# Embedding look-ups as fp32r matmuls over a table in two parts, with moved transposes and partial sums

## The chip, the cores and the metric

The kernel runs on one core of a Trainium2 chip. The metric is the device time of one execution in microseconds. The engines are TensorE (PE, matmuls into PSUM), VectorE (DVE), ScalarE (ACT), GpSimd (POOL, which also issues the gathers) and SyncE (SP, which issues the other transfers). Each runs its own instructions in order and waits on semaphores for the others.

## The reference

A recommendation tower over B = 512 samples: 40 look-ups in tables of 64 columns, one bilinear form for each of the 780 pairs of fields, then three dense layers. Cut to what matters:

```python
e = jnp.stack([tbl_0[ids[:, 0]], ..., tbl_39[ids[:, 39]]], axis=1)      # 512 x 40 x 64
vi, vj = e[:, i_idx, :], e[:, j_idx, :]                                 # 780 pairs i < j
z = jnp.einsum('bpe,bpe->bp', jnp.einsum('bpd,pde->bpe', vi, W), vj)    # 512 x 780
h = jnp.concatenate([z, dense_ctx], axis=1)                             # 512 x 796
h = jnp.maximum(h @ W_top1 + b_top1, 0.0)
h = jnp.maximum(h @ W_top2 + b_top2, 0.0)
y = h @ W_top3
```

## The kernel before

Fields are taken in 20 pairs; `x[:, k, :]` holds pair k transposed, one field in the lower 64 partitions, the other in the upper 64, samples along the free axis. Eight fields with tables of 1000 rows are the one-hot fields, pairs 0, 2, 4, 6. The rest are gathered: GpSimd issues 8 gathers a pair (two fields by four blocks of 128 samples, L396), with a memset of `spacer` (L391) and a wait for it between any two, and TensorE transposes the four blocks into PSUM (L559).

A one-hot look-up (`look`, L533 to L545) multiplies the table, in 8 blocks of 128 rows, with a one-hot matrix. VectorE makes that matrix by comparing the ids, copied to all partitions, with the row numbers (`make_rows`, L472, L484; 8 comparisons a field, two fields together). The two fields of a pair go to the two halves of the columns, so 16 matmuls of 128x64 by 512 in fp32. `one_hot` holds one pair.

Work on the forms is a list of 195 steps (`UNITS`): for k = 1, 2, ... all pairs m < k with k (`cross`, L606), some `inner` ones (L612), and from k = 8 on `rows` units (L595) which serve the pairs in `KEPT` from the other side. A step is two matmuls of 64 rows side by side into one of three `y_ps` slots, a product on VectorE with `x[:, k]` (L518) or `kept` (L504), and for every four summed steps a sum over partitions on TensorE three steps later (`sum_round`, L629). A product of a `rows` unit is summed by ScalarE in 16 activations (`sum_rows`, L440).

The order is written out. `plan_jobs` gives each step the jobs that come before it on every engine: `look`, `turn` (transposes), `mix` (ScalarE swaps halves for an inner unit), `partial` (the first layer's sum over z banks already finished, L574) and `z_turn`. `EARLY_JOBS` places the first ones by hand, the others stand `LEAD` = 5 steps ahead of their first use; `FIRST` is {5: 11, 6: 16, 7: 22, 8: 30, 9: 36, 10: 44, 11: 52} for these pairs. `ROWS_AT` places the comparisons on VectorE, ahead of a step's product. The results of jobs land in banks of `y_ps` for those of step 0 (`TURN_BANK`) and later in the one bank `t_ps`; the next job there waits until the last is copied out, by ScalarE (`copy_turn`, L409) or, for the second group of partial sums, by VectorE (L491):

```python
if TURN_BANK[n] in TURN_BANK[:n]:
    wait_turn_done(pe, max(i for i in range(n) if TURN_BANK[i] == TURN_BANK[n]))
```

In step 84 stand the transposes of pair 14 and partial sum (0, 0) together. SyncE loads ids and tables of the one-hot fields, 256 KB each, then chunks of weights.

## Time and profile before

| | |
|---|---|
| median of 3 runs | 351.81 us (351.06 to 351.86) |
| the profiled execution, its own time | 351.51 us |
| its span, first to last instruction | 349.7 us |
| TensorE busy | 331.0 us, 95% |
| VectorE busy | 258.4 us, 74% |
| ScalarE busy | 220.7 us, 63% |
| GpSimd busy | 153.8 us, 44% |
| granted TensorE clock | 1.00 |

Busy time of TensorE is that of matmuls whose ends are modelled: a busy engine isn't one at its peak. 1.8 us of the execution lie outside the span.

### The profile page before, as it was taken

The numbers are of one execution on the slowest core, as the hardware profiler recorded it, in microseconds if no ns is written. First come the engines' busy times: TensorE is split into PE (matmuls) and PEld (weight loads), VectorE is DVE, ScalarE is ACT, GpSimd is POOL, SyncE is SP. The second block draws the span as 40 slices with busy tenths as digits, with TensorE's granted clock in tenths as the row PEclk, the third lists the DMA queues.
The fourth block names the chain that finished last, engine by engine and source line by source line (L and its number), as shares of the span: only waits on it lengthen the run. The fifth ranks groups of instructions, "written<-read, shape, count | busy, mean of one in ns | idle before, by whom it ended". The sixth has DMA issues, their size and how long they took to land.

```text
span 349.7 us, 5874 instructions
## 1 busy us (share of the span) xinstructions
PE 331.0 (95%) x1664; PEld 112.4 (32%) x1664; DVE 258.4 (74%) x271; ACT 220.7 (63%) x1595; POOL 153.8 (44%) x261
## 2 busy tenths in 40 slices
PE   0999879999999999997999999999999999999997
PEld 0333223333333333332333333333333333333342
DVE  3967599177798789894578788998878988777230
ACT  1010400120499999996997899999999897663032
POOL 2888888888865856562254444452441000000000
PEclk9999999999999999999999999999999999999999
DMA  6941121312212131732030303122121100000000
GB/s 190 408 173 24 24 82 47 121 25 85 83 49 74 25 109 35 297 93 90 8 107 10 104 14 97 34 86 72 43 73 34 63 0 3 0 0 3 0 1 0
DMA packets 12323, 24.37 MB, mean 70 GB/s; under 512 B 3953, under 2 KB 3953, under 8 KB 12162
## 3 DMA queue, kind: packets, MB, share of 16 engines
q1 hardware_dynamic: 8194, 19.79, 16.1%
q0 software_dynamic: 4096, 4.20, 5.1%
q8 instruction: 13, 0.21, 0.3%
q14 instruction: 20, 0.16, 0.2%
HBM read 23.98 MB, written 0.00 MB: 69 GB/s over the span
## 4 chain that ended last, share of the span: by engine, by line
PE 92%; ACT 2%; DVE 2%; DMA 1%; issue 1%; SPq 1%; DVEq 0%
PE y_ps L606 37%; PE z_ps L629 19%; PE y_ps L595 13%; PE t_ps L540 7%; PE t_ps L574 4%; PE y_ps L641 3%; PE t_ps L559 2%; PE y_ps L671 2%; PE y_ps L540 2%; DMA table<-in_small_tables 1%; PE y_ps L612 1%; ACT row_prod L440 1%; DVE one_hot L484 1%; DVE prod L518 1%; ACT x L409 1%
## 5 line engine op out<-in xcount | busy, mean ns | idle before, releaser
L518 DVE TENSOR_TENSOR prod<-y_ps,x 128x1024 f32<-128x1024 f32 x142 | 168.0, 1216 | 47.3 <-PE y_ps L606 47.0
L440 ACT ACTIVATE row_prod<-row_prod 128x64 f32<-128x64 f32 x768 | 183.5, 242 | 12.0 <-DVE row_prod L504 11.9
L606 PE MATMUL y_ps<-x,w_sb 64*128 64x512 f32 x568 | 144.5, 613 | 5.1 <-ACT x L409 2.3
L440 ACT ACTIVATION_READ_ACCUMULATOR row_prod<-row_prod 128x1 f32 x768 | 144.5, 188 | 0.0
L396 POOL DMA_INDIRECT rows<-in_tbl,ids_sb x96 | 91.3, 951 | 96.6 <-PE y_ps L606 46.5
L606 PEld LDWEIGHTS y_ps<-x,w_sb 64*128 64x128 f32 x568 | 49.1, 185 | 87.7 <-issue 41.5
L629 PE MATMUL z_ps<-prod,selector 128*32 128x512 f32 x588 | 71.2, 598 | 0.0
L504 DVE TENSOR_TENSOR row_prod<-y_ps,kept 128x1024 f32<-128x1024 f32 x48 | 58.4, 1217 | 14.3 <-PE y_ps L595 14.3
L409 ACT ACTIVATE x<-t_ps 128x512 f32<-128x512 f32 x18 | 10.6, 588 | 72.8 <-PE t_ps L540 38.9
L595 PE MATMUL y_ps<-w_rows_sb,x 64*128 64x512 f32 x192 | 51.5, 612 | 0.0
L396 POOL DMA_INDIRECT kept<-in_tbl,ids_sb x32 | 31.4, 981 | 13.7 <-POOL spacer L391 8.4
L629 PEld LDWEIGHTS z_ps<-prod,selector 128*32 128x32 f32 x588 | 15.4, 109 | 50.3 <-issue 40.4
L484 DVE TENSOR_SCALAR one_hot<-x,numbers 128x512 f32<-128x512 int32 x64 | 27.9, 507 | 4.6 <-DMA x<-in_ids_one_hot 4.6
L540 PE MATMUL t_ps<-one_hot,table 128*64 128x512 f32 x96 | 23.1, 637 | 8.2 <-DMA table<-in_small_tables 8.2
L391 POOL MEMSET spacer<- 128x128 f32 x127 | 30.5, 240 | 0.1
L595 PEld LDWEIGHTS y_ps<-w_rows_sb,x 64*128 64x128 f32 x192 | 16.5, 186 | 26.1 <-issue 13.7
L574 PE MATMUL t_ps<-z_sb,w_sb 128*128 128x512 f32 x32 | 15.9, 618 | 2.5 <-ACT x L409 2.5
L540 PEld LDWEIGHTS t_ps<-one_hot,table 128*64 128x64 f32 x96 | 7.3, 147 | 22.8 <-issue 22.2
L426 ACT ACTIVATE x_mix<-x 64x512 f32<-64x512 f32 x20 | 12.6, 629 | 0.5
L431 ACT ACTIVATE z_sb<-z_ps 128x512 f32<-128x512 f32 x5 | 3.0, 599 | 12.5 <-PE z_ps L629 12.5
L641 PE MATMUL y_ps<-z_sb,w_sb 128*128 128x512 f32 x24 | 10.8, 601 | 0.0
L529 DVE TENSOR_TENSOR partial_sb<-y_ps,partial_sb 128x512 f32<-128x512 f32 x3 | 2.1, 692 | 10.6 <-PE y_ps L641 10.6
(40 smaller groups left out, 79.2 us busy)
## 6 DMA issues: line engine op xcount, KB each, us to landing
w_sb<-in_w_units SPq DMA_DIRECT2D x19, 512.0 KB, 3.8
w_rows_sb<-in_w_rows SPq DMA_DIRECT2D x12, 256.0 KB, 2.8
x<-in_ids_one_hot SPq DMA_DIRECT2D x8, 256.0 KB, 4.8
table<-in_small_tables SPq DMA_DIRECT2D x8, 256.0 KB, 5.2
w_sb<-in_w SPq DMA_DIRECT2D x1, 1792.0 KB, 7.7
rows<-in_tbl,ids_sb POOLq DMA_INDIRECT x96, 2.4
kept<-in_tbl,ids_sb POOLq DMA_INDIRECT x32, 2.4
w_sb<-in_w SPq DMA_DIRECT2D x1, 512.0 KB, 4.5
```

The source lines that it names most:

```text
L391: pool.memset(spacer[:], 0.0).then_inc(spaced, 1)
L396: pool.indirect_dma_start(rows_ap(n, bt)[:, h * D:(h + 1) * D], None, tables[f], bass.IndirectOffsetOnAxis(ap=ids_sb[:, bt, f:f + 1], axis=0),
L440: ins = act.activation(own, own, ACT.Copy, accum_out=z_rows[:, bt, column:column + 1])
L484: ins = dve.tensor_scalar(one_hot[:, h, k, :], ids_all[:, 2 * n + h, :], numbers[:, k:k + 1], None, ALU.is_equal)
L504: dve.tensor_tensor(row_prod[:, n % ROW_PROD_SLOTS], y_ps[:, s % Y_SLOTS], leaf, ALU.mult).then_inc(prod_ready, 1)
L518: dve.tensor_tensor(prod[:, at:at + 2, :], y_ps[:, s % Y_SLOTS], leaf, ALU.mult).then_inc(prod_ready, 1)
L540: ins = pe.matmul(dst[D * h:D * h + D, :], table[:, n, h, k, :], one_hot[:, h, k, :], start=(k == 0), stop=(k == TK - 1))
L574: ins = pe.matmul(dst, w1_sb[:, b, P * m:P * m + P], z_sb[:, b, :], start=(b % 2 == 0), stop=(b % 2 == 1))
L595: ins = pe.matmul(y_ps[:, slot, h, :], x[own, k, P * bt:P * bt + P], w_rows_sb[own, (k - ROWS_FROM) % ROW_W_SLOTS, :], start=True, stop=True)
L606: ins = pe.matmul(y_ps[:, slot, h, :], w_sb[own, c % W_SLOTS, at:at + P], x[own, m, :], start=True, stop=True)
L629: ins = pe.matmul(z_ps[q:q + 32, :], selector[:, 30 - row - 2 * n:62 - row - 2 * n], prod[:, 2 * (u % G_UNITS) + n, :], start=(n == 0 and ...
L641: return pe.matmul(h1_ps[m], w1_sb[:, b, P * m:P * m + P], z_sb[:, b, :], start=(b == EARLY_BANKS), stop=(b == BANKS - 1))
```

## The change

- The table of a one-hot field is taken apart into a high part (ScalarE copies it to fp32r, `high_table`) and a low part (GpSimd subtracts the high one from the table, `low_table`), side by side in the 128 columns of `table_parts`. The one-hot matrix is fp32r too.
- A look-up is made for each field: 8 matmuls over 128 columns in fp32r, whose result has the high part in the field's own half and the low part in the other. ScalarE copies the high half to `x`, VectorE adds the low one (`add_low`).
- `one_hot` and `table_parts` are rings by field (2 and 4 places); the comparisons, the additions and the look-ups have new places (`EARLY_DVE`, `EARLY_JOBS`). The first two low parts are made whole ahead of gather 1, the others in quarters of two blocks ahead of gathers 2 to 17, in place of the spacer and its wait (`EARLY_POOL`: two quarters each ahead of gathers 2 to 9, one each ahead of 10 to 17).
- Ids and tables are loaded field by field; the number and size of the transfers stay.
- The transposes of pairs 9, 10 and 11 stand 3 steps ahead of their use instead of 5 (steps 33, 41, 49 instead of 31, 39, 47).
- A partial sum keeps four steps away from transposes: those of group 0 stand in steps 88, 92, 102, 106 instead of 84, 88, 92, 96; group 1 is unchanged.

```diff
-EARLY_JOBS = {0: [("look", 0), ("look", 2), ("turn", 1)], 3: [("look", 4), ("turn", 3)], 11: [("turn", 5)],
-              16: [("look", 6)]}
+LATE, LATE_LEAD = (9, 10, 11), 3
+EARLY_JOBS = {0: [("look", 0), ("look", 1), ("look", 4), ("look", 5), ("turn", 1)], 1: [("look", 8)],
+              2: [("look", 9)], 3: [("turn", 3)], 11: [("turn", 5)], 12: [("look", 12)], 14: [("look", 13)]}
-TK_STEP = 2
-TK_STEPS = TK // TK_STEP
-ROWS_AT = {0: [(n, i) for n in range(2) for i in range(TK_STEPS)] + [(2, 0), (2, 1)], 1: [(2, 2)], 2: [(2, 3)],
-           4: [(3, 0)], 7: [(3, 1)], 10: [(3, 2)], 13: [(3, 3)]}
+ROW_HALF = TK // 2
+EARLY_DVE = {0: [("rows", 0, 0), ("rows", 0, 1), ("rows", 1, 0), ("rows", 1, 1), ("rows", 2, 0), ("rows", 2, 1),
+                 ("low", 0), ("rows", 3, 0), ("low", 1), ("rows", 3, 1), ("rows", 4, 0), ("low", 4), ("rows", 4, 1),
+                 ("low", 5)],
+             1: [("rows", 5, 0)], 2: [("low", 8), ("rows", 5, 1)], 3: [("low", 9)],
+             4: [("rows", 6, 0)], 6: [("rows", 6, 1)], 8: [("rows", 7, 0)], 10: [("rows", 7, 1)],
+             13: [("low", 12)], 15: [("low", 13)]}
+EARLY_POOL = {1: [(0, 0, TK), (1, 0, TK)],
+              **{2 + i: [(2 + i // 2, 4 * (i % 2) + j, 4 * (i % 2) + j + 2) for j in (0, 2)] for i in range(4)},
+              **{6 + i: [(4 + i // 2, 4 * (i % 2) + j, 4 * (i % 2) + j + 2) for j in (0, 2)] for i in range(4)},
+              **{10 + i: [(6 + i // 4, 2 * (i % 4), 2 * (i % 4) + 2)] for i in range(8)}}
+LOW_PARTS = [sum(first < TK and f <= n for at in EARLY_POOL.values() for f, first, _ in at) for n in range(8)]
 PARTIAL_PAIRS = 2
...
     for k in range(EARLY_PAIRS, NP):
-        jobs_at[FIRST[k] - LEAD].append(("turn", k))
+        jobs_at[FIRST[k] - (LATE_LEAD if k in LATE else LEAD)].append(("turn", k))
     for q, s in INNER_AT.items():
...
     for pair in range(PARTIAL_PAIRS):
-        start = SUMMED[ROUND * BANK_ROUNDS * 2 * (pair + 1) - 1] + SUM_LAG + 3
+        at = SUMMED[ROUND * BANK_ROUNDS * 2 * (pair + 1) - 1] + SUM_LAG + 3
         for m in range(M1):
-            jobs_at[start + PARTIAL_EVERY * m].append(("partial", pair, m))
+            while any(job[0] == "turn" for jobs in jobs_at[at - PARTIAL_EVERY + 1:at + PARTIAL_EVERY] for job in jobs):
+                at += 1
+            jobs_at[at].append(("partial", pair, m))
+            at += PARTIAL_EVERY
     jobs_at[ROWED[BT * GROUPS_IN_BANK - 1] + 8].append(("z_turn", 0))
...
-ON_DVE = [job[0] == "partial" and job[1] > 0 for job in TURNS]
+ON_DVE = [job[0] == "look" or (job[0] == "partial" and job[1] > 0) for job in TURNS]
 LOOKS = [job[1] for job in TURNS if job[0] == "look"]
...
-        with nc.sbuf_tensor("one_hot", [P, 2, TK, B], F32) as one_hot, \
-                nc.sbuf_tensor("table", [P, len(LOOKS), 2, TK, D], F32) as table:
+        with nc.sbuf_tensor("one_hot", [P, 2, TK, B], F32R) as one_hot, \
+                nc.sbuf_tensor("table", [P, 4, TK, D], F32) as table, \
+                nc.sbuf_tensor("table_parts", [P, 4, TK, 2 * D], F32R) as table_parts:
             pass
...
         t_ps = ps("t_ps", [P, B])[:]
+        def table_ap(n):
+            return table[:, n, :, :] if n < 4 else x[:, NP - len(LOOKS) - 8 + n, :].rearrange("p (k d) -> p k d", d=D)
...
+            def load_field(n):
+                sp.dma_start(ids_all[:, n, :], ids_one_hot[n:n + 1, :].to_broadcast([P, B])).then_inc(looked_loaded[n], 16)
+                sp.dma_start(table_ap(n), small_tables[n]).then_inc(table_loaded[n], 16)
             sp.dma_start(numbers[:], row_numbers).then_inc(numbers_loaded, 16)
-            load_ids(0)
+            load_field(0)
             sp.dma_start(ids_sb[:], ids.rearrange("(t p) f -> p t f", p=P)).then_inc(ids_loaded, 16)
-            load_tables(0)
-            load_ids(1)
-            load_tables(1)
+            for n in range(1, 4):
+                load_field(n)
             load_weights(0)
-            for n in range(2, len(LOOKS)):
-                load_ids(n)
-                load_tables(n)
+            for n in range(4, len(LOOKS)):
+                load_field(n)
             for c in range(1, CHUNKS):
...
                                pattern=[[-1, P]], channel_multiplier=1).then_inc(ident_ready, 1)
+            def low_table(n, first, to):
+                own, other = slice(D * (n % 2), D * (n % 2) + D), slice(D - D * (n % 2), P - D * (n % 2))
+                parts = table_parts[:, n % 4, first:to, :]
+                pool.wait_ge(table_high, n + 1)
+                pool.tensor_tensor(parts[:, :, other], table_ap(n)[:, first:to, :], parts[:, :, own].bitcast(F32),
+                                   ALU.subtract).then_inc(table_low, 1)
             pool.wait_ge(ids_loaded, 16)
...
                     f = ORDER[2 * k + h]
-                    if (at := 2 * BT * n + i) > 0:
+                    if (at := 2 * BT * n + i) in EARLY_POOL:
+                        for job in EARLY_POOL[at]:
+                            low_table(*job)
+                    elif at > 0:
                         pool.memset(spacer[:], 0.0).then_inc(spaced, 1)
-                        pool.wait_ge(spaced, at)
+                        pool.wait_ge(spaced, at - sum(g < at for g in EARLY_POOL))
                     if k >= PACED_FROM:
...
         def _(act):
+            def high_table(n):
+                if n >= 4:
+                    act.wait_ge(turned, TURN_SEQ["look", LOOKS[n - 4]] + 1)
+                act.wait_ge(table_loaded[n], 16)
+                own = slice(D * (n % 2), D * (n % 2) + D)
+                act.activation(table_parts[:, n % 4, :, own], table_ap(n), ACT.Copy).then_inc(table_high, 1)
             def copy_turn(job):
...
                 act.wait_ge(turned, n + 1)
-                if job[0] in ("look", "turn"):
+                if job[0] == "look":
+                    k, h = divmod(job[1], 2)
+                    own = slice(D * h, D * h + D)
+                    act.activation(x[own, k, :], turn_ps(n)[own, :], ACT.Copy).then_inc(high_copied, 1)
+                elif job[0] == "turn":
                     act.activation(x[:, job[1], :], turn_ps(n), ACT.Copy).then_inc(turn_on_act, 1)
...
+            for n in range(4):
+                high_table(n)
             for s in range(STEPS):
...
                         copy_turn(job)
+                        if job[0] == "look" and LOOKS.index(job[1]) + 4 < len(LOOKS):
+                            high_table(LOOKS.index(job[1]) + 4)
                 if (r := round_at(s)) is not None and r % BANK_ROUNDS == BANK_ROUNDS - 1:
...
-            def make_rows(n, step):
-                if n == 0 and step == 0:
+            def make_rows(n, half):
+                if n == 0 and half == 0:
                     dve.wait_ge(numbers_loaded, 16)
-                if step == 0:
-                    dve.wait_ge(looked_loaded[n], 32)
-                if n > 0 and step < TK_STEPS - 1:
-                    dve.wait_ge(one_hot_used, (TK_STEPS - 1) * (n - 1) + step + 1)
-                elif n > 0:
-                    dve.wait_ge(turned, TURN_SEQ["look", LOOKS[n - 1]] + 1)
-                for k in range(TK_STEP * step, TK_STEP * step + TK_STEP):
-                    for h in range(2):
-                        ins = dve.tensor_scalar(one_hot[:, h, k, :], ids_all[:, 2 * n + h, :],
-                                                numbers[:, k:k + 1], None, ALU.is_equal)
+                if half == 0:
+                    dve.wait_ge(looked_loaded[n], 16)
+                if n >= 2 and half == 0:
+                    dve.wait_ge(one_hot_used, n - 1)
+                elif n >= 2:
+                    dve.wait_ge(turned, TURN_SEQ["look", LOOKS[n - 2]] + 1)
+                for k in range(ROW_HALF * half, ROW_HALF * half + ROW_HALF):
+                    ins = dve.tensor_scalar(one_hot[:, n % 2, k, :], ids_all[:, n, :],
+                                            numbers[:, k:k + 1], None, ALU.is_equal)
                 ins.then_inc(one_hot_made, 1)
+            def add_low(p):
+                k, h = divmod(p, 2)
+                own, other = slice(D * h, D * h + D), slice(D - D * h, P - D * h)
+                dve.wait_ge(high_copied, LOOKS.index(p) + 1)
+                dve.tensor_tensor(x[own, k, :], turn_ps(TURN_SEQ["look", p])[other, :], x[own, k, :],
+                                  ALU.add).then_inc(turn_on_dve, 1)
...
             for s in range(STEPS):
-                for n, step in ROWS_AT.get(s, ()):
-                    make_rows(n, step)
+                for job in EARLY_DVE.get(s, ()):
+                    if job[0] == "rows":
+                        make_rows(*job[1:])
+                    else:
+                        add_low(job[1])
                 for job in JOBS_AT[s]:
...
         def _(pe):
-            def look_up(pair, dst):
-                n = LOOKS.index(pair)
-                pe.wait_ge(table_loaded[n], 32)
+            def look_up(p, dst):
+                n = LOOKS.index(p)
+                pe.wait_ge(table_low, LOW_PARTS[n])
                 for k in range(TK):
-                    if k % TK_STEP == 0:
-                        pe.wait_ge(one_hot_made, TK_STEPS * n + k // TK_STEP + 1)
-                    for h in range(2):
-                        ins = pe.matmul(dst[D * h:D * h + D, :], table[:, n, h, k, :], one_hot[:, h, k, :],
-                                        start=(k == 0), stop=(k == TK - 1))
-                    if k == TK - 1:
-                        ins.then_inc(turned, 1)
-                    elif k % TK_STEP == TK_STEP - 1:
+                    if k % ROW_HALF == 0:
+                        pe.wait_ge(one_hot_made, 2 * n + 1 + k // ROW_HALF)
+                    ins = pe.matmul(dst, table_parts[:, n % 4, k, :], one_hot[:, n % 2, k, :],
+                                    start=(k == 0), stop=(k == TK - 1))
+                    if k == ROW_HALF - 1:
                         ins.then_inc(one_hot_used, 1)
+                ins.then_inc(turned, 1)
...
                 n = TURN_SEQ[job]
```

## Rows read from the trace of the kernel before

**Rows 1.** Busy time of each engine by stretch of the span, with TensorE's granted clock
```profile
0.00:26.00 26.00, 17.11 (x72) 6.37 (x74) 17.46 (x44) 3.06 (x4) 16.88 (x29) 1.00 0.72 259
...
40.00:60.00 20.00, 17.23 (x102) 5.34 (x102) 19.38 (x28) 0.60 (x1) 16.47 (x27) 1.00 0.18 50
...
80.00:160.00 80.00, 79.99 (x443) 26.88 (x444) 67.22 (x60) 65.06 (x498) 52.35 (x90) 1.00 0.31 101
...
166.00:300.00 134.00, 133.94 (x700) 44.98 (x698) 110.11 (x96) 122.78 (x948) 39.52 (x67) 1.00 0.16 49
...
sum 349.70, PE 331.04 PEld 112.44 DVE 258.39 ACT 220.68 POOL 153.85; mean PE 41.38 PEld 14.06 DVE 32.30 ACT 27.58 POOL 19.23
```

**Rows 2.** Timeline of VectorE, first 70 us: start, duration, instructions, idle before
```profile
6.26 16.80 DVE L484 TENSOR_SCALAR one_hot<-x,numbers 128x512 f32<-128x512 int32 x40 [4.64 <-DMA x<-in_ids_one_hot]
26.50 1.23 DVE L518 TENSOR_TENSOR prod<-y_ps,x 128x1024 f32<-128x1024 f32 x1 [3.44 <-PE y_ps L606]
...
38.90 1.23 DVE L518 TENSOR_TENSOR prod<-y_ps,x 128x1024 f32<-128x1024 f32 x1 [5.43 <-PE y_ps L606]
...
47.07 3.47 DVE L518 TENSOR_TENSOR prod<-y_ps,x 128x1024 f32<-128x1024 f32 x3
50.47 1.70 DVE L484 TENSOR_SCALAR one_hot<-x,numbers 128x512 f32<-128x512 int32 x4
52.09 1.20 DVE L518 TENSOR_TENSOR prod<-y_ps,x 128x1024 f32<-128x1024 f32 x1
...
68.38 1.23 DVE L518 TENSOR_TENSOR prod<-y_ps,x 128x1024 f32<-128x1024 f32 x1 [6.82 <-PE y_ps L606]
```

**Rows 3.** Timeline of TensorE's matmuls, posts of four stretches
```profile
23.87 0.65 PE L559 MATMUL y_ps<-ident,kept 128*128 128x128 f32 x4
...
28.04 7.09 PE L540 MATMUL t_ps<-one_hot,table 128*64 128x512 f32 x32
35.82 0.66 PE L559 MATMUL t_ps<-ident,kept 128*128 128x128 f32 x4 [0.70 <-ACT x L409]
...
48.34 1.13 PE L606 MATMUL y_ps<-x,w_sb 64*128 64x512 f32 x4 [1.74 <-DVE prod L518]
...
52.69 3.70 PE L606 MATMUL y_ps<-x,w_sb 64*128 64x512 f32 x16 [0.78 <-ACT x L409]
...
67.11 1.13 PE L606 MATMUL y_ps<-x,w_sb 64*128 64x512 f32 x4 [0.79 <-ACT x L409]
...
107.14 2.96 PE L606 MATMUL y_ps<-x,w_sb 64*128 64x512 f32 x12
110.04 0.66 PE L559 MATMUL t_ps<-ident,rows 128*128 128x128 f32 x4
...
163.73 1.98 PE L574 MATMUL t_ps<-z_sb,w_sb 128*128 128x512 f32 x4 [2.50 <-ACT x L409]
```

**Rows 4.** Timeline of GpSimd: its select, first, eighth and 64th gather
```profile
1.19 0.28 POOL L378 TENSOR_SCALAR_AFFINE_SELECT ident<-ident 128x128 f32<-128x128 f32 x1 [0.24 <-POOL ident L376]
6.82 1.29 POOL L396 DMA_INDIRECT kept<-in_tbl,ids_sb  x1 [5.35 <-DMA ids_sb<-in_ids]
...
18.83 1.00 POOL L396 DMA_INDIRECT kept<-in_tbl,ids_sb  x1 [0.27 <-POOL spacer L391]
...
101.37 0.95 POOL L396 DMA_INDIRECT rows<-in_tbl,ids_sb  x1 [0.27 <-POOL spacer L391]
```

**Rows 5.** Groups by line and shape: the addition out of PSUM
```profile
L529 DVE TENSOR_TENSOR partial_sb<-y_ps,partial_sb 128x512 f32<-128x512 f32 x3 | 2.1, 692 | 10.6 <-PE y_ps L641 10.6
```

**Rows 6.** Timeline of ScalarE around the copy of pair 10
```profile
101.78 0.57 ACT L409 ACTIVATE x<-t_ps 128x512 f32<-128x512 f32 x1
```

**Rows 7.** The line of the spacer: minimum, median, maximum in ns
```profile
L391 POOL MEMSET spacer<- x127: 218/218/410, 8.1 to 260.8; 128x128 f32 x127
```

**Rows 8.** DMA issues: count, median us from issue to landing
```profile
kept<-in_tbl,ids_sb POOLq DMA_INDIRECT x32, 2.4
```

**Rows 9.** Chain that ended last, 155 to 168 us
```profile
159.39 3.81 ACT row_prod L440 x32
163.20 0.49 ACT x L409
```

18 lines of the change are left out of this document (8 added, 10 removed).

## Prediction

> **What bounds the kernel now.** I first read the busy times by stretch. TensorE is busy for 331.04 of 349.70 us, at a granted clock of 1.00, which is 2.4 GHz. The stretches show that this average hides three parts. From 80 us on TensorE has no gap (79.99 of 80 us, 133.94 of 134) but one of 2.50 us at 163.73 us [rows 1, 3]. Before 60 us it isn't the only bound: in the first 26 us it works for 17.11 us, and between 40 and 60 us VectorE is the fuller engine with 19.38 of 20 us [rows 1]. So time taken from TensorE before 60 us counts only if VectorE and the gathers can follow; the end moves by what the product of step 16 moves, since from there TensorE runs without a gap.
>
> The timeline of VectorE gives the posts of this start: comparisons from 6.26 us, first product (step 0) at 26.50, step 3 at 38.90, step 10 at 52.09 to 53.29, step 16 at 68.38 us after 6.82 us of idling behind the fourth look-up [rows 2]. The timeline of TensorE gives those that answer to them [rows 3], and that of GpSimd the gathers [rows 4].
>
> **Prices.** A comparison takes 0.42 us (16.80 / 40), a product 1.14 us from start to start (three from 47.07 to 50.47), a group of four comparisons 1.62 us at 50.47 to 52.09 [rows 2]; beside a spacer they last longer, and I take 1.77. An addition out of PSUM of 128x512 takes 0.69 us [rows 5]; I take 0.65 for the new one of 64x512. ScalarE's copy is 0.57 to 0.6 us [rows 6]. A gather's issue holds GpSimd for 1.0 us, with its spacer (0.41 beside comparisons, 0.22 alone) and the wait for it (0.27) 1.68 or 1.44 us, and lands 2.4 us after its start [rows 4, 7, 8].
>
> **Part 1, looks on TensorE.** Before, a pair costs 32 records in 7.09 us, 28 us for four pairs [rows 3]. Now it is two fields of 8 matmuls over the whole width of 128x512. What one costs in fp32r no row shows. Above stands the fp32 matmul of that shape: two in 1.98 us, chained, so at most 0.99 each [rows 3]. Below stands one column per cycle at 2.4 GHz, 512 / 2.4 = 0.21 us; four times that is 0.85, so fp32 pays for four passes and a lead. The code splits each entry in two parts of fewer bits, so I read one pass as meant and take 0.25 us, a look-up of a field 2.0 us and a pair 4.0. The saving is 28 - 16 = 12 us of TensorE. The Trainium skill ("FP8 and Floating Point Precision", TensorE Precision Notes) says that true FP32 takes four passes and that a reduced precision reads four bytes truncated; by it the look-up would be a quarter of the fp32 matmul's time, and no trace of the kernel before can test it.
>
> **Part 2, making the parts.** ScalarE's eight high parts (0.6 us each) and its eight copies instead of four lie in a stretch where it is busy for 3.06 of 26 us [rows 1]: nothing. Without that cover each would add 0.6 us to its look-up. GpSimd's subtractions aren't hidden: they stand in the gather queue. No row shows a two-input operation on GpSimd. The nearest is its select over 128x128, 0.28 us with one input [rows 4]; double that is the upper end. A spacer of the same size is stretched from 0.22 to 0.41 beside comparisons [rows 7], so a quarter table (two of its eight blocks, 128x128) is 0.28 + 0.19 = 0.47 us and a whole one 4 x 0.28 + 0.19 = 1.3 us. Gather 0 ends at 8.12 us, two wholes take it to 10.7, gather 1 ends at 11.7. Each of the next six is 2 x 0.47 + 1.0 = 1.94 us (before 1.68), so gather 7 starts at 11.7 + 5 x 1.94 + 0.94 = 22.3 us (before 18.83) and lands at 24.7. From the transposes of pair 1 to the first product it was 26.50 - 23.87 = 2.63 us [rows 2, 3]: this path allows the first product at 27.4 us.
>
> VectorE must now do in step 0 as many comparisons as before, 6.26 + 16.8 = 23.1 us, and four additions: 25.7 us. On top comes what GpSimd takes from it. The memsets pressed between its comparisons didn't slow them (pitch 0.42 with and without), so some 0.2 us of GpSimd fits in; what goes beyond I let push VectorE: 0.93 for each whole table and 0.08 for each of 12 quarters, 2.8 us. The first product comes at about 28.5 us, 2.0 later than before. Ends: 25.7 us (nothing pushed, quarters at 0.28) and 34 us (two inputs at double price: quarters 0.75 and wholes 2.45 put gather 7's landing at 30.4 and pushes 2 x 2.06 + 12 x 0.36 = 8.4 us on VectorE).
>
> **Part 3, steps 0 to 16 walked through.** Product 0 to 29.7, four comparisons to 31.4, product 1 to 32.6, addition of field 8 to 33.2, four comparisons to 35.0. Look-up 9 needs these last rows: half of it, 1.0 us, then 1.27 from matmul to product (67.11 to 68.38): product 2 from 37.3 to 38.4, addition 9 to 39.1. Only then is t_ps free for the transposes of pair 3 (new order: look-up, addition on VectorE, transposes), and 3.08 us behind their start (35.82 to 38.90) product 3 starts, at 42.2 us: 3.3 late. Gather 15 has landed: 23.3 + 2 x 1.94 + 5 x 1.47 + 0.47 + 2.4 = 37.4 us. Steps 3 to 10 are VectorE's alone, with four groups of comparisons now instead of three: 14.39 + 1.77 = 16.2 us, product 10 ends at 58.4 (5.1 late). Now TensorE leads again. Cross 10 starts behind product 7, 6.96 us before that end, at 51.5; as before, 4.35 us later (48.34 to 52.69) cross 11 at 55.9; look-up 12 from 56.7 to 58.7; cross 12; product 12 and addition 12 to 61.9, since look-up 13 needs t_ps; look-up 13 to 64.0; cross 14, the sum of a round (1.85), cross 15: cross 16 at 67.6 us, where before it stood at 67.11. The start gives back all it saves: +0.5 us. The saved 12 us of TensorE went into a later first product (2.0), the two handovers of t_ps in steps 2 and 3 (1.3), one more group of comparisons in the VectorE stretch (1.8), the rest into new waits around look-ups 12 and 13 and into the idling of TensorE in the first 28 us.
>
> **Part 4, the partial sums.** Before, transposes of pair 14 and partial sum (0, 0) both lie in step 84 and use t_ps. Its copy on ScalarE is queued behind 16 row sums until 163.20, and TensorE sits idle for 2.50 us [rows 3, 9]. With the sum four steps later, a step being at least 0.86 us and usually 1.1 with its share of a round's sum, a copy that waits behind one block of row sums (3.81 us [rows 9]) is done in time. The others keep four steps from any transpose too. Gain 2.5 us, carried to the end since TensorE has no gap from 166 to 300 us [rows 1]. Work isn't added.
>
> **Part 5, transposes of pairs 9 to 11 two steps later.** Their gathers start later by what GpSimd lost: gather 7 by 3.5 us, then up to 3.7. The last of pair 11 started at 101.37 and would land at 107.5, against transposes at 110.04 before [rows 3, 4]; so with the old lead it would still be in time, and the move buys nothing but a margin. Its cost: pair 10's copy now stands behind one more block of row sums. That block began after the old copy, 102.4, and by its 3.81 us ends at 106.2; without the copy ahead of it the new copy ends there too, and cross(0, 10) is due at about 107.1 [rows 3, 6]. Nothing, with 0.9 us to spare.
>
> **Sum.** +0.5 - 2.5 = -2.0 us on the profiled 351.51 us, that is 349.5 us. The median of the runs shown is 0.3 us above that execution; I leave that in the range.
>
> **Rivals.** (a) GpSimd is cheap: nothing pushed, first product at 25.7, 2.8 us earlier than in my walk; all posts move: about 346.7 us. For it speaks that memsets cost VectorE nothing; against it, that a subtraction reads as well. Chance 0.17.
>
> (b) GpSimd holds VectorE for the subtraction's whole length, 12 x 0.28 + 2 x 1.13 = 5.6 us instead of 2.8: 352.3 us, no difference. The spacers' 0.41 against 0.22 us shows that one waits for the other; the pitch of 0.42 shows that it isn't mutual for short ones. The Trainium skill ("SBUF — State Buffer", Who interferes with whom) makes it an exclusive lock for a whole instruction, which is this rival. The trace agrees for GpSimd's side alone. Chance 0.13.
>
> (c) The other side: the two-input price doubles. Then the first product is at 34 us, 5.5 later, gather 15 lands at 45.9 and holds the transposes of pair 3 another 1.2 us: about 356 us, slower. It decides from a first product at 30.5 us on (28.5 plus the 2.0 of gain). GpSimd's select and memset, 0.28 and 0.22 for the same size, differ little by the added input; that speaks against it. Chance 0.10.
>
> (d) fp32r takes two or four passes. At two, 0.43 each, half of look-up 9 and look-ups 12 and 13 add 0.7 + 1.4 + 1.4: 353 us. At four the looks are 55 us and the end lies near 375. Chance 0.08.
>
> (e) Comparisons that write fp32r lose their rate. They run at 0.42 us where an addition of as many elements needs 0.69 [rows 5]; 0.2 us on each of 64 gives about 362 us. Chance 0.05.
>
> (f) The wait around t_ps moves only: pair 10's copy, or a partial sum's, meets another block of row sums, and the 2.5 us stay: 352.0 us. Chance 0.09.
>
> My own forecast, 347.7 to 350.7 us, keeps 0.38.
>
> **The numbers.** A measurement of this kernel can tell about 0.3%, 1.05 us, so faster means under 350.75. Faster is my forecast and (a): 0.55. Within 0.3% are (b), (f): 0.22. Slower are (c), (d), (e): 0.23. The range runs from 346 us (just below (a)) to 354 us, which takes in (b), (f) and (d) at two passes; outside lie (c), (e), (d) at four passes, less than 0.2.
>
> **What the profile would show.** Matmuls of the look-ups 0.2 to 0.3 us apart (0.4 or more would be (d)); comparisons still 0.42 apart where GpSimd doesn't subtract; subtractions of 0.3 to 0.5 and 1.1 to 1.4 us; first product at 28 to 29 us and cross 16 at 67 to 68.5; no idle TensorE around 160 us. A first product before 26.5, or waits for gathers at pairs 3 and 9 to 11, would make the sum wrong; so would a look-up 12 that starts earlier than 56 us because VectorE ran ahead.

## The result, and the profile after

The changed kernel takes 357.62 us (median of 4 runs, 356.41 to 358.24) against 351.84 us for the kernel before in the same comparison: a ratio of 1.014, 95% interval [1.009, 1.019]. It is slower by 5.8 us, where 2 us faster was forecast, and it lies outside the range of 346 to 354 us. The profiled execution took 358.24 us, its span is 356.4 us instead of 349.7.

VectorE's timeline after, which answers to [rows 2] (L527 comparisons, L535 the new addition, L568 products; left out are the additions and groups between):

```profile
4.77 15.58 DVE L527 TENSOR_SCALAR one_hot<-x,numbers 128x512 fp32r<-128x512 int32 x24 [3.15 <-DMA x<-in_ids_one_hot]
...
50.03 1.22 DVE L568 TENSOR_TENSOR prod<-y_ps,x 128x1024 f32<-128x1024 f32 x1 [3.42 <-PE y_ps L657]
...
55.33 1.76 DVE L527 TENSOR_SCALAR one_hot<-x,numbers 128x512 fp32r<-128x512 int32 x4
...
65.29 2.33 DVE L568 TENSOR_TENSOR prod<-y_ps,x 128x1024 f32<-128x1024 f32 x2
...
76.31 4.86 DVE L568 TENSOR_TENSOR prod<-y_ps,x 128x1024 f32<-128x1024 f32 x4 [0.98 <-PE y_ps L657]
```

The comparisons begin 1.5 us earlier than before, but stand 0.65 us apart (15.58 / 24) instead of 0.42. At 55.33, when GpSimd no longer subtracts, four take 1.76 us, within the 1.70 to 1.97 of before, though they still write fp32r. The first product comes at 32.75 us, 6.25 late; step 3 at 50.03, 11.1 late; the product of step 15 is the first of the last row, so step 16 follows at 77.45 us, 9.1 late. The groups by line, up to 33 us, show the same for all forty, and what GpSimd did meanwhile:

```profile
L527 DVE TENSOR_SCALAR one_hot<-x,numbers 128x512 fp32r<-128x512 int32 x40 | 24.8, 690 | 3.2 <-DMA x<-in_ids_one_hot 3.2
L568 DVE TENSOR_TENSOR prod<-y_ps,x 128x1024 f32<-128x1024 f32 x1 | 1.2, 1226 | 0.4 <-PE y_ps L657 0.4
...
L402 POOL TENSOR_TENSOR table_parts<-table,table_parts 128x128 fp32r<-128x128 f32 (+1 forms) x10 | 7.0, 715 | 0.1
L402 POOL TENSOR_TENSOR table_parts<-x,table_parts 128x128 fp32r<-128x128 f32 x11 | 6.0, 555 | 0.1
```

Forty comparisons hold VectorE for 24.8 us instead of 16.8, beside 13.0 us of subtractions. GpSimd's timeline gives their lengths, 1.25 us for a whole table and 0.56 for a quarter, to set beside [rows 4]:

```profile
7.48 2.50 POOL L402 TENSOR_TENSOR table_parts<-table,table_parts 128x512 fp32r<-128x512 f32 x2
...
11.12 1.12 POOL L402 TENSOR_TENSOR table_parts<-table,table_parts 128x128 fp32r<-128x128 f32 x2
...
23.66 0.96 POOL L424 DMA_INDIRECT kept<-in_tbl,ids_sb  x1 [0.15 <-issue]
```

TensorE's timeline after (L592 looks, L610 transposes, L657 crosses, L625 partial sums), beside [rows 3]:

```profile
30.57 2.08 PE L657 MATMUL y_ps<-x,w_sb 64*128 64x512 f32 x4 [1.15 <-issue]
...
38.85 1.19 PE L592 MATMUL t_ps<-one_hot,table_parts 128*128 128x512 f32 x4 [2.12 <-DVE x L535]
...
46.66 0.66 PE L610 MATMUL t_ps<-ident,kept 128*128 128x128 f32 x4 [2.04 <-DVE x L535]
48.10 4.54 PE L657 MATMUL y_ps<-x,w_sb 64*128 64x512 f32 x12 [0.78 <-ACT x L449]
...
55.45 1.13 PE L657 MATMUL y_ps<-x,w_sb 64*128 64x512 f32 x4
...
64.81 2.12 PE L592 MATMUL t_ps<-one_hot,table_parts 128*128 128x512 f32 x8
...
142.90 1.13 PE L657 MATMUL y_ps<-x,w_sb 64*128 64x512 f32 x4 [0.51 <-ACT x L449]
...
174.51 1.92 PE L680 MATMUL z_ps<-prod,selector 128*32 128x512 f32 x16
176.36 1.98 PE L625 MATMUL t_ps<-z_sb,w_sb 128*128 128x512 f32 x4
```

A cross product takes 2.08 us at 30.57 and 1.13 at 55.45: the same instructions, at about half the rate. The windows, 10 us each, tell why; the column behind the busy times is the granted clock:

```profile
20.00:30.00 10.00, 5.29 (x16) 3.38 (x16) 9.87 (x18) 2.46 (x5) 9.14 (x15) 0.73 0.16 47
30.00:40.00 10.00, 7.31 (x20) 3.70 (x20) 8.69 (x14) 1.06 (x2) 8.94 (x13) 0.76 0.11 22
40.00:50.00 10.00, 6.22 (x19) 2.80 (x20) 2.86 (x4) 3.13 (x6) 8.27 (x14) 0.75 0.11 20
50.00:60.00 10.00, 9.16 (x48) 2.78 (x45) 9.96 (x15) 0.57 (x1) 8.29 (x13) 0.91 0.28 77
```

TensorE works for 5.29 of 10 us from 20 us on, where it worked for 9.27 before, and its granted clock, which stood at 1.00 in every stretch of [rows 1], is between 0.73 and 0.91 over 40 us: parts at 2.4 and parts at 1.2 GHz. VectorE then idles for TensorE, 3.42 us ahead of the product at 50.03.

The end can be accounted for. From product 16 on the idle time of 2.50 us at 163.73 [rows 3] is gone, as the rows at 174.51 and 176.36 show: the partial sum follows the sum of a round without a gap. So the span should be 349.7 + (77.45 - 68.38) - 2.5 = 356.3 us; it is 356.4. The 2.5 hides two things, though. From product 16 to the end it takes 279.0 us instead of 281.3, and TensorE has a wait that it did not have before, 0.51 us at 142.90; where it comes from is told with the experiments on the two moves.

### The profile page after: what moved, and what is told of

Its sections match the earlier page's. It is cut to its first block, busy times and chain, and to the rows that moved or that the text cites. A ratio compares the mean times of both kernels' runs of the same rounds, so it can differ in the third digit from the quotient of the medians.

```text
span 356.4 us, 5787 instructions
## 1 busy us (share of the span) xinstructions
PE 328.9 (92%) x1600; PEld 118.2 (33%) x1600; DVE 273.0 (77%) x279; ACT 227.8 (64%) x1607; POOL 163.5 (46%) x270
## 4 chain that ended last, share of the span: by engine, by line
PE 81%; DVE 10%; ACT 6%; issue 2%; DMA 1%; SPq 0%; DVEq 0%
PE y_ps L657 35%; PE z_ps L680 18%; PE y_ps L646 12%; DVE one_hot L527 7%; PE t_ps L625 4%; ACT row_prod L480 4%; PE y_ps L692 3%; PE t_ps L592 2%; PE t_ps L610 2%; PE y_ps L722 2%; DVE prod L568 2%; DMA x<-in_ids_one_hot 1%; PE y_ps L663 1%; DVE x L535 1%; ACT x_mix L466 1%
## 5 line engine op out<-in xcount | busy, mean ns | idle before, releaser
L568 DVE TENSOR_TENSOR prod<-y_ps,x 128x1024 f32<-128x1024 f32 x142 | 168.3, 1216 | 41.1 <-PE y_ps L657 40.7
L657 PE MATMUL y_ps<-x,w_sb 64*128 64x512 f32 x568 | 148.7, 627 | 4.1 <-ACT x L449 2.1
L657 PEld LDWEIGHTS y_ps<-x,w_sb 64*128 64x128 f32 x568 | 49.9, 189 | 85.1 <-issue 39.4
L527 DVE TENSOR_SCALAR one_hot<-x,numbers 128x512 fp32r<-128x512 int32 x64 | 36.8, 641 | 3.2 <-DMA x<-in_ids_one_hot 3.2
L449 ACT ACTIVATE x<-t_ps 128x512 f32<-128x512 f32 x15 | 8.8, 589 | 43.5 <-PE t_ps L610 43.5
L592 PE MATMUL t_ps<-one_hot,table_parts 128*128 128x512 f32 x40 | 14.2, 501 | 13.7 <-POOL table_parts L402 8.9
L419 POOL MEMSET spacer<- 128x128 f32 x110 | 24.8, 226 | 0.1
L447 ACT ACTIVATE x<-t_ps 64x512 f32<-64x512 f32 x5 | 3.0, 592 | 21.4 <-PE t_ps L592 21.4
L625 PE MATMUL t_ps<-z_sb,w_sb 128*128 128x512 f32 x32 | 15.9, 618 | 0.0
L592 PEld LDWEIGHTS t_ps<-one_hot,table_parts 128*128 128x128 f32 x40 | 8.8, 238 | 20.3 <-issue 9.6
L592 PE MATMUL y_ps<-one_hot,table_parts 128*128 128x512 f32 x24 | 9.7, 539 | 5.4 <-DVE one_hot L527 5.3
```

The source lines that it names most:

```text
L419: pool.memset(spacer[:], 0.0).then_inc(spaced, 1)
L527: ins = dve.tensor_scalar(one_hot[:, n % 2, k, :], ids_all[:, n, :], numbers[:, k:k + 1], None, ALU.is_equal)
L568: dve.tensor_tensor(prod[:, at:at + 2, :], y_ps[:, s % Y_SLOTS], leaf, ALU.mult).then_inc(prod_ready, 1)
L592: ins = pe.matmul(dst, table_parts[:, n % 4, k, :], one_hot[:, n % 2, k, :], start=(k == 0), stop=(k == TK - 1))
L625: ins = pe.matmul(dst, w1_sb[:, b, P * m:P * m + P], z_sb[:, b, :], start=(b % 2 == 0), stop=(b % 2 == 1))
L657: ins = pe.matmul(y_ps[:, slot, h, :], w_sb[own, c % W_SLOTS, at:at + P], x[own, m, :], start=True, stop=True)
```

## The experiments

The kernels ran in four groups, each group on one chip with its own runs of the kernel before. On the chip of the second group (fill, fill without subtraction, subtractions in before, pair 3 in the z bank) the kernel before itself takes 360.5 us, and in the profiles of all four VectorE and ScalarE stand still for some us between 86 and 105 us, so of these four I use ratios and times before 80 us. The letters of theories in an expectation are its own group's.

### Parts of the change alone

**The kernel before, with its partial sums moved as in the change** (the `while` loop of the change's `partial` placement, nothing else).

> The kernel before with only the partial sums moved away from transposes (steps 88, 92, 102, 106 for group 0). Theory (the wait around t_ps is all that this part touches): TensorE's idle 2.50 us at 163.7 us is gone and nothing else moves, so about 349.3 us, 0.7% faster. Rival (the copy that was late meets another block of row sums): the idle time comes back at one of the new places, 351 to 352 us.

Measured: 348.64 us against 352.61, ratio 0.989 [0.984, 0.993]; repeated in the fourth group 349.02 against 351.87, 0.989 [0.984, 0.994]. TensorE's timeline has no idle time left there:

```profile
164.12 1.92 PE L633 MATMUL z_ps<-prod,selector 128*32 128x512 f32 x16
165.98 1.98 PE L578 MATMUL t_ps<-z_sb,w_sb 128*128 128x512 f32 x4
```

It beats both kernels. From product 16 to the end its profile takes 278.3 us, as does that of the repetition: 3.0 less than before, of which 2.5 are the wait. The repetition:

> The kernel before with the partial sums moved alone, beside the others on one chip: ratio 0.985 to 0.993, as e1. If e12's way were as good, it would stand at 0.996 or above here; expected is that it stays 2 us or more below e12's ratio.

**The same, with the transposes of pairs 9 to 11 later too.**

```diff
-        jobs_at[FIRST[k] - LEAD].append(("turn", k))
+        jobs_at[FIRST[k] - (3 if k in (9, 10, 11) else LEAD)].append(("turn", k))
```

> The kernel before with the partial sums moved and also the transposes of pairs 9 to 11 two steps later. Theory (the later transposes are hidden work with a margin): the same time as with the partial sums alone, within 0.3 us, about 349.3 us. Rival (the copy of pair 10, now behind one more block of row sums, holds cross(0, 10)): 0.5 to 1 us slower than the partial sums alone, with TensorE idle near 107 us.

Measured: 349.78 us, ratio 0.990 [0.987, 0.993], 1.1 us above the median of the partial sums alone. The intervals overlap, but the profile has a wait that neither the kernel before nor that with the partial sums alone has:

```profile
134.08 1.13 PE L610 MATMUL y_ps<-x,w_sb 64*128 64x512 f32 x4 [0.50 <-ACT x L413]
```

This is cross(0, 12), waiting for the copy of pair 12, whose transposes weren't moved: ScalarE starts that copy 5.3 us after the start of its transposes, at 133.36 us, where with the partial sums alone it is 4.6 us. From product 16 to the end it takes 279.1 us instead of 278.3. The changed kernel has the same wait (0.51 us at 142.90), and the one without the later transposes, which follows, doesn't. So they cost 0.5 us of waiting and 0.8 in all: the size that the rival named, at another place than the 107 us that it named.

**The changed kernel without either move** (`LATE = ()`, partial sums in their old steps).

> The changed kernel with partial sums and transposes of pairs 9 to 11 back at their old steps: the look-ups in two parts alone. Theory (the loss lies in the first 78 us, where the changed kernel's step 16 was 9 us late, and the moved partial sums gave 2.5 us of it back): about 360 us, 2.5 us more than the changed kernel. Rival (the later transposes cost something after the late start): less than 2 us more than the changed kernel.

Measured: 361.16 us, ratio 1.024 [1.018, 1.030]; its span of 358.9 us is 2.5 above that of the changed kernel, and TensorE's waits name the old one: 2.5 us for t_ps, on ScalarE. Of these 2.5 us, 0.4 lie before product 16 (77.85 us against 77.45); behind it the two moves together are worth 2.1, the wait less what the later transposes cost. All of the loss of the change is in the look-ups.

### What the subtractions cost

**The low part left out.** Both halves of `table_parts` are filled with the high part by ScalarE, GpSimd's memsets are back in place of the subtractions. Each looked-up value is thus twice its high part; the work on TensorE and VectorE is that of the changed kernel.

```diff
-EARLY_POOL = {1: [(0, 0, TK), (1, 0, TK)], ...}
+EARLY_POOL = {}
...
+                act.activation(table_parts[:, n % 4, :, other], table_ap(n), ACT.Copy).then_inc(table_low, 1)
```

> The changed kernel without the subtraction on GpSimd: ScalarE copies the table to both halves of table_parts, and GpSimd has its spacers back; the low part is left out (both halves hold the high one). Theory A (GpSimd's subtractions block VectorE's comparisons and delay gathers; the low clock of TensorE is a consequence of its waiting for them): comparisons 0.42 us apart again, first product at 25 to 26.5 us instead of 32.75, clock near 1.00, about 347 to 349 us. Theory B (TensorE has too little work in the first 50 us whoever prepares it, so its clock falls anyway): comparisons at 0.42 but the granted clock still at half for 10 us or more, product of step 3 at 43 us or later, 351 to 354 us.

Measured: 352.41 us, ratio 0.998 [0.995, 1.002]. VectorE's timeline and three windows:

```profile
4.79 10.02 DVE L526 TENSOR_SCALAR one_hot<-x,numbers 128x512 fp32r<-128x512 int32 x24 [3.17 <-DMA x<-in_ids_one_hot]
...
26.68 1.22 DVE L567 TENSOR_TENSOR prod<-y_ps,x 128x1024 f32<-128x1024 f32 x1 [1.90 <-PE y_ps L656]
```

```profile
20.00:30.00 10.00, 7.82 (x22) 4.46 (x24) 7.59 (x15) 2.60 (x5) 8.37 (x13) 0.66 0.21 59
30.00:40.00 10.00, 5.14 (x20) 2.18 (x16) 5.51 (x8) 1.09 (x3) 8.10 (x15) 0.96 0.14 25
40.00:50.00 10.00, 9.43 (x42) 3.29 (x44) 7.24 (x12) 2.94 (x5) 8.10 (x15) 0.70 0.10 21
```

The comparisons are back at 0.42 us (10.02 / 24), while writing fp32r. The clock falls all the same, to 0.66 and 0.70 in two windows. So there are two causes, and neither is the comparisons' type. Each theory had one of them.

**The kernel before with GpSimd's subtractions added**: 28 of 128x128 on scratch, in place of the memsets ahead of gathers 1 to 17, nothing in fp32r.

```diff
+                            pool.tensor_tensor(scratch[:, len(made) % 8, :], ident[:], ident[:],
+                                               ALU.subtract).then_inc(scratched, 1)
```

> The kernel before, its fp32 look-ups untouched, with 28 two-input subtractions of 128x128 on GpSimd (identity minus identity, into a scratch tile) in place of the spacers of gathers 1 to 17: four, eight times two, eight times one. Theory (the two engines exclude each other for a whole instruction): the first 40 comparisons take 22 to 24 us instead of 16.8 with TensorE still at clock 1.00, first product 4 to 6 us later, and some of it hidden behind TensorE later: 354 to 357 us. Rival (the comparisons of the changed kernel are slow because they write fp32r): the comparisons keep 0.42 us and the time stays within 1 us of before.

Measured: ratio 1.014 [1.009, 1.018], as large a loss as the whole change's, but it comes about in another way. The timelines of VectorE, GpSimd and TensorE, and two windows:

```profile
6.09 20.96 DVE L495 TENSOR_SCALAR one_hot<-x,numbers 128x512 f32<-128x512 int32 x40 [4.47 <-DMA x<-in_ids_one_hot]
28.91 1.23 DVE L529 TENSOR_TENSOR prod<-y_ps,x 128x1024 f32<-128x1024 f32 x1 [1.86 <-PE y_ps L617]
```

```profile
8.49 2.25 POOL L397 TENSOR_TENSOR scratch<-ident 128x128 f32<-128x128 f32 x4
```

```profile
26.21 0.66 PE L570 MATMUL y_ps<-ident,kept 128*128 128x128 f32 x4 [1.44 <-DMA kept<-in_tbl,ids_sb]
27.59 4.54 PE L617 MATMUL y_ps<-x,w_sb 64*128 64x512 f32 x12 [0.73 <-issue]
```

```profile
28.00:30.00 2.00, 2.00 (x8) 1.03 (x6) 1.08 (x1) 0.00 (x0) 1.83 (x3) 0.63 0.12 25
30.00:32.00 2.00, 2.00 (x6) 0.40 (x2) 2.00 (x5) 0.00 (x0) 1.82 (x4) 0.52 0.10 16
```

Comparisons in plain fp32 lose their rate as well, 0.52 us each. Forty lose 4.2 us here; in the changed kernel they lose 8.0. Why the factor differs (whole tables, strided halves of `table_parts`, other data) was not tried.

What this lost rate costs, the run doesn't show. The comparisons end at 27.05 us, and the first product waits until 28.91 for TensorE, whose transposes of pair 1 waited 1.44 us for the last of their gathers. So the first product is 2.4 us late by the gathers, which GpSimd issues later. In the changed kernel no such wait stands: its transposes at 28.36 us follow the look-up at once, and gather 7 was issued at 23.66. The clock of 1.00 that I had expected wasn't kept either: three cross products take 4.54 us instead of 2.85, with TensorE's own work as before. Product 16 comes at 73.98 us, 5.6 late, of which about 2.3 are the gathers and 3.3 the clock.

### What the clock costs

**Filling TensorE's idle stretches** in the changed kernel: matmuls of the identity with itself, 128 columns in fp32, into the z bank before anything is summed there.

```diff
+FILL_BEFORE = {('look', 5): 7, ('look', 9): 8, ('turn', 3): 8}
+FILL_INSIDE = {4: 3, 5: 8, 9: 3}
...
+            def fill(count):
+                for _ in range(count):
+                    pe.matmul(z_ps[:, 0:P], ident[:], ident[:], start=True, stop=True)
```

> The changed kernel with small fp32 matmuls (identity by identity, 128 columns, into z_ps ahead of its first use) in the places where TensorE waits between 19 and 47 us; all its own work stays. Theory (TensorE's clock at half costs 4 to 6 us of the first 50): the granted clock stays at 1.00, cross units take 1.1 instead of 2.1 us, and the time falls from 357.6 to 352 to 354 us. Rival (VectorE sets the pace there and the low clock is hidden by it): the clock is at 1.00, but the time falls by less than 1 us.

> The kernel without subtraction (both halves hold the high part, the low one is left out), with the same kind of filling matmuls. Theory (subtraction and clock are the two losses, and they add up): clock 1.00, 3 to 4 us less than the 352.4 us without filling, 348.5 to 349.5 us, so no better than the kernel before with its partial sums moved. Rival (the handovers of t_ps over VectorE set the time whatever the clock): 351 to 352.4 us.

The number of fills follows each kernel's gaps: 37 here, 36 with the low part left out, 30 in a later kernel.

Measured: filled, ratio 1.011 [1.007, 1.015], granted clock 1.00 in the first 80 us; the 352 to 354 us expected would have been a ratio of up to 1.006. Filled and with the low part left out, 0.988 [0.982, 0.993], as expected, though the clock fell to 0.90 and 0.93 in the two windows from 40 to 60 us. To have it beside the changed kernel on one chip, I ran both again:

> The changed kernel as it is, as the one that the next three are read against on the same chip. Both theories: 1.4% over the kernel before (ratio 1.01 to 1.02), first product near 32.75 us, the product ahead of step 16 near 76.3 us, cross product 3 to 4 us late by a granted clock of 0.5 in parts of 24 to 52 us.

> The changed kernel with filling matmuls in TensorE's idle stretches ahead of step 10. Theory A (the loss is the clock and the subtractions, and what is won ahead of step 16 is kept to the end): granted clock 1.00 in the first 80 us, product ahead of step 16 near 71.9 us, whole time 3.5 to 5 us below the changed kernel of this call. Rival (TensorE's later work takes the gain back, because a later wait is set by something else): less than 1.5 us below.

Measured: changed 358.0 us (357.5 to 359.2), ratio 1.018 [1.010, 1.025]; filled 356.1 (354.8 to 356.6), ratio 1.009 [1.005, 1.013]. That is 1.9 less, where 3.5 to 5 was expected and under 1.5 by the rival: between the two. In the filled kernel's profile the clock fell at a place that I hadn't filled (windows of 2 us):

```profile
54.00:56.00 2.00, 0.88 (x4) 0.30 (x4) 2.00 (x2) 0.00 (x0) 1.73 (x4) 1.00 0.64 250
56.00:58.00 2.00, 2.00 (x6) 0.32 (x4) 2.00 (x5) 0.00 (x0) 1.52 (x3) 0.62 0.14 27
58.00:60.00 2.00, 2.00 (x14) 0.58 (x16) 2.00 (x3) 0.00 (x0) 1.66 (x3) 0.53 0.19 33
```

The executions of the filled kernel whose mean clock was 1.00 took 354.8 and 354.9 us, those with a lower one 355.4 to 356.6. The kept clock is thus worth about 3 us, and even the filled kernel doesn't always keep it.

**Pair 3's transposes in the z bank**, so that they needn't wait for the addition out of t_ps (idle 2.04 us at 46.66), first in the changed and then in the filled kernel.

```diff
+            if TURNS[n] == ("turn", 3):
+                return z_ps[:]
```

> The changed kernel with the transposes of pair 3 into z_ps, free until the first sum of a round, so that they don't wait for VectorE's addition of field 9 in t_ps. Theory (this handover costs 1.2 to 2 us and everything behind it is VectorE's): 1.5 to 3 us less than the changed kernel, 355 to 356 us. Rival (TensorE's clock or VectorE takes the place of the wait): less than 0.7 us.

> The filled kernel, and the turn of pair 3 in the z bank, so that its look-up need not wait for the bank of pair 2. Theory A (with the clock kept, what is left is VectorE's late comparisons and not the bank): 0 to 1 us below the filled kernel. Rival (the bank is the chain's own wait): products 2 and 3 of the chain stand 2 to 3 us apart in place of 4.7, and the whole time is 2 us or more below the filled kernel.

Measured: ratio 1.009 [1.006, 1.011], with the product of step 15 at 75.34 us, against 76.31 and 75.64 in the two profiles of the changed kernel; filled, 355.0 us against 356.1, and that product at 73.15 us, against 71.85, 73.04 and 74.78 in the three profiles of the filled kernel. So the bank brought about 1 us. In neither profile was the clock kept (0.67 from 20 to 50 us in the first, 0.90 and 0.93 in the two windows from 30 to 50 in the filled one), so what the bank brings at a clock of 1.00 isn't shown.

### The two causes apart

**The eight subtractions on VectorE**, 128x512 each, ahead of its comparisons, GpSimd's memsets back; filled, and later the same without filling.

```diff
+                dve.tensor_tensor(parts[:, :, other], table_ap(n), parts[:, :, own].bitcast(F32),
+                                   ALU.subtract).then_inc(table_low, 1)
```

> The filled kernel with the subtractions of the low parts on VectorE as eight 128x512 subtractions ahead of its comparisons, and GpSimd's fills back in their places. Theory A (what costs is that the two engines shut each other out while GpSimd reads two inputs, not the work itself): the comparisons go back to 0.42 us, the eight subtractions cost VectorE 8 x 0.69 = 5.5 us, as much as the lockout did, so the whole time is within 1.5 us of the filled kernel. Rival (GpSimd's own lateness of gathers is the cost): 3 us or more below the filled kernel.

> The subtractions on VectorE, GpSimd's fills back in place, no filling matmuls. Theory: without the fill the granted clock falls to 0.5 again in parts of 20 to 50 us and the product of step 15 is 2 to 4 us later than e12's 68.89 us (ratio 1.00 to 1.01). Rival (the clock is worth under 1 us on the path, the shut-out nearly all): product of step 15 within 1 us of 68.89 us, ratio near 0.996.

Measured: filled 350.77 us, ratio 0.996 [0.992, 1.000], 5.3 us below the filled kernel. I had expected no more than 1.5, holding the lockout to cost as much as the work itself; it costs more. The rival had named 3 us or more, for another reason, late gathers. The filled kernel's profile speaks against that reason: no wait of TensorE there names a gather, gather 7 is issued at 23.86 us and the transposes of pair 1 follow the last look-up at 28.05; gather 15 is issued at 38.26 and the transposes of pair 3 run at 44.38. Not filled: 353.93 us, ratio 1.006 [1.003, 1.009]. VectorE's timeline, filled, then two windows of the one that isn't:

```profile
6.49 0.68 DVE L535 TENSOR_TENSOR table_parts<-table,table_parts 128x512 fp32r<-128x512 f32 x1
7.09 3.39 DVE L527 TENSOR_SCALAR one_hot<-x,numbers 128x512 fp32r<-128x512 int32 x8
...
27.90 1.22 DVE L575 TENSOR_TENSOR prod<-y_ps,x 128x1024 f32<-128x1024 f32 x1
...
68.89 4.86 DVE L575 TENSOR_TENSOR prod<-y_ps,x 128x1024 f32<-128x1024 f32 x4 [0.97 <-PE y_ps L672]
```

```profile
20.00:30.00 10.00, 8.33 (x19) 4.82 (x20) 8.99 (x18) 1.82 (x3) 8.37 (x13) 0.50 0.19 55
...
40.00:50.00 10.00, 8.34 (x36) 3.14 (x40) 6.09 (x10) 3.11 (x5) 8.10 (x15) 0.66 0.14 24
```

A subtraction costs VectorE 0.6 us of its own time. GpSimd needs the same table's four quarters, 2.2 us. Two more on the chip of the last group, filled with the low part left out, and filled:

> As e6: the low parts left out and TensorE's idle stretches filled. Theory (two causes, the clock and the shut-out): first product near 25.6 us, product of step 15 near 67.1 us, ratio near 0.988, 2.0 to 2.8% below the filled kernel of this call. Rival (the clock falls later and takes it back): ratio 0.995 or more, with a granted clock under 1 after 50 us.

> The changed kernel filled, a third time, to stand beside e13. Theory: first product between 31 and 32.6 us, product of step 15 between 71.9 and 74.8 us by whether the granted clock falls once near 56 us, ratio 1.009 to 1.011. Rival (the gain of filling is only the chip's own spread): product of step 15 at 75.5 us or later.

Measured: 347.76 us (0.989 [0.985, 0.994]) and 355.24 (1.011 [1.006, 1.016]), both with a clock of 1.00. VectorE's posts, without the low part and then with GpSimd's subtractions:

```profile
25.06 1.23 DVE L569 TENSOR_TENSOR prod<-y_ps,x 128x1024 f32<-128x1024 f32 x1 [0.24 <-PE y_ps L664]
...
38.73 1.23 DVE L569 TENSOR_TENSOR prod<-y_ps,x 128x1024 f32<-128x1024 f32 x1 [2.73 <-PE y_ps L664]
...
64.75 4.86 DVE L569 TENSOR_TENSOR prod<-y_ps,x 128x1024 f32<-128x1024 f32 x4 [0.97 <-PE y_ps L664]
```

```profile
32.46 1.23 DVE L570 TENSOR_TENSOR prod<-y_ps,x 128x1024 f32<-128x1024 f32 x1
...
46.97 1.23 DVE L570 TENSOR_TENSOR prod<-y_ps,x 128x1024 f32<-128x1024 f32 x1 [2.73 <-PE y_ps L665]
...
73.04 4.86 DVE L570 TENSOR_TENSOR prod<-y_ps,x 128x1024 f32<-128x1024 f32 x4 [0.97 <-PE y_ps L665]
```

Put together, with the span worked out as above, 349.7 + (product of step 15 + 1.14 - 68.38) - 2.5:

| subtractions | filled | first product | step 3 | step 15 | span worked out | span measured |
|---|---|---|---|---|---|---|
| GpSimd | no | 32.75 | 50.03 | 76.31 | 356.3 | 356.4 |
| GpSimd | yes | 32.46 | 46.97 | 73.04 | 353.0 | 353.1 |
| VectorE | no | 28.78 | 44.71 | 71.42 | 351.4 | 351.5 |
| VectorE | yes | 27.90 | 42.22 | 68.89 | 348.9 | 349.0 |
| none | no | 26.68 | 42.76 | 69.22 | 349.2 | 349.3 |
| none | yes | 25.06 | 38.73 | 64.75 | 344.7 | 344.8 |

All that differs is settled by the product of step 15: behind product 16 all six take 278.9 to 279.0 us. With the clock kept, GpSimd's subtractions cost 8.3 us and VectorE's 4.1; the clock costs 2.5 to 4.5 us in each pair. The rows are single profiles from several chips, and one kernel's profiles differ: the changed kernel's second has the product of step 15 at 75.64, the filled kernel's other two at 71.85 and, with the clock fallen near 56 us, at 74.78. By the 71.85 the subtractions on GpSimd cost 7.1 us, so I take these for good to about 1 us.

## Why the prediction was wrong

**Part 1 was right in its price, and said nothing of what else it did.** Eight matmuls of a look-up take 2.12 us at 64.81, 0.26 each, where 0.25 was assumed, so rival (d) falls. By the Trainium skill ("FP8 and Floating Point Precision", TensorE Precision Notes) true FP32 takes four passes, so that a single pass would take about a quarter, an estimate; 0.26 against at most 0.99 agrees. But the time taken off TensorE between 20 and 50 us didn't stay a mere surplus: with 5.3 to 7.3 of 10 us of work the granted clock fell to half in parts of it. No step of the sum, and no rival, had the clock at another level than the 1.00 of [rows 1]; the price of a falling clock was put at nothing, without a reason. That is the mechanism I missed altogether. The filled kernels show it: the same kernel with useless matmuls in the gaps is about 3 us faster. What opens the gaps can be either part of the change: without subtractions the clock fell too (0.66 and 0.70), and so it did with the fp32 look-ups untouched and GpSimd late.

**Part 2, the prices right, the push wrong.** A quarter table takes 0.56 us (0.47 assumed), a whole one 1.25 (1.3), and gather 7 starts at 23.66 (22.3). What failed is the sentence that "what goes beyond I let push VectorE: 0.93 for each whole table and 0.08 for each of 12 quarters, 2.8 us". It pushed 8.0 us (24.8 - 16.8). I had taken the memsets, beside which the comparisons keep 0.42 us on average, for the measure of what a subtraction leaves alone (even beside memsets a group of four takes 1.97 us at 27.64 and 1.70 at 50.47 [rows 2], a difference that isn't explained). And I counted 12 quarters where 19 had started before the first product. First product: 28.5 forecast, + 5.2 of push, - 1.5 as the comparisons began at 4.77 instead of 6.26 (ids are loaded field by field now), + 0.5 for the rest (0.44 is the wait for the cross product) is 32.7; it is 32.75. This is rival (b)'s mechanism at more than rival (c)'s threshold of 30.5. Rival (c)'s own reason, a doubled price, did not come true. The Trainium skill ("SBUF — State Buffer", Who interferes with whom) gives the pair of ports that the two engines share to whichever comes first, and blocks the other for the whole instruction. The trace agrees as to the direction: VectorE lost 8.0 us beside 13.0 us of subtractions. As to the amount it can't tell, since the listed length of a subtraction may hold GpSimd's own waiting: on scratch, one of 128x128 is listed with 0.41 us where VectorE rests and with 0.50 beside comparisons. Rival (a) is excluded, and so is (e): comparisons writing fp32r keep 0.42.

**Part 3, the walk.** Against its own stretches, it held except between the first product and step 3:

| stretch | walk | changed | filled, none subtracted |
|---|---|---|---|
| first product to step 3 | 13.7 | 17.3 | 13.7 |
| step 3 to end of product 10 | 16.2 | 16.4 | 16.0 |
| from there to product 16 | 10.5 | 11.0 | 11.2 |

(Product 10 is the first of the two at 65.29 in the changed kernel; its end is 66.4 with 1.14 us. The walk's cross 16 at 67.6 is product 16 at 68.9.) The sum of misses is 4.25 + 3.6 + 0.2 + 0.5 = 8.55 us, which is 77.45 - 68.9. Of the 3.6, 2.8 are the clock: filled, with GpSimd's subtractions, the stretch takes 14.5 us. Had the subtractions been free and the clock kept, product 16 would have stood at 65.9 us, 2.5 ahead of before: that is all that 12 us less work on TensorE could bring.

**Part 4 was right in its mechanism and a little small**: the wait of 2.5 us is gone, and in the kernel before alone the move takes 3.0 us off the stretch behind product 16 (4.0 and 2.9 us between medians, whose intervals hold both figures); what the other 0.5 us are stays open. Rival (f), that the whole wait comes back, didn't happen. **Part 5 was wrong by 0.5 to 0.8 us**: it looked at cross(0, 10) alone and found 0.9 us to spare, but the copy of pair 12, behind later copies and row sums on ScalarE, holds cross(0, 12) for 0.5 us. Part 5's loss and the surplus of part 4 nearly cancel, so that the -2.5 of the sum met the measured -2.4 by luck.

**The sum**: forecast +0.5 - 2.5. Measured, +9.1 at product 16 and -2.4 behind it, +6.7, as the spans differ. The step that failed is the +0.5 of parts 2 and 3: a push of 2.8 us on VectorE that measured 8.0, and the clock, put at nothing, that cost 2.5 to 4.5.

## What to carry to other kernels

Ask of an operation that is moved to GpSimd not how long it takes there but how long VectorE stands still for it: here eight subtractions were cheaper on the full VectorE (4.1 us of end) than on GpSimd (7 to 8 us), and memsets say nothing about two-input operations. When work is taken off TensorE in a stretch that another engine bounds, look at whether the granted clock will survive the gaps that this makes; the saved time was worth 2.5 us at best, the lost clock took about 3. And try the small repair by itself: moving four partial sums away from a transpose gave 1.1%, and was hidden inside a change that cost 1.4%. Each small move wants such a run: the later transposes, held to be free because one wait had been checked, cost 0.5 us at another.
